# Attention's maxima and score products cut into eight tiles of 64 rows by 32 columns

## What is computed

```python
q = (x @ Wq.T + bq).reshape(Bb, Nn, H, hd).transpose(0, 2, 1, 3)
k = (x @ Wk.T + bk).reshape(Bb, Nn, H, hd).transpose(0, 2, 1, 3)
...
a1 = jax.nn.softmax(jnp.einsum('bhnd,bhmd->bhnm', q1, k1) * scale, axis=-1)
x1 = jnp.einsum('bhnm,bhmd->bhnd', a1, v1).transpose(0, 2, 1, 3).reshape(Bb, Nn, C // 2)
...
out = jnp.concatenate([x1 - lv * x2, x2], axis=-1) @ Wp.T + bp
```

## Time and profile before

| what | value |
|---|---|
| median of 3 runs | 4907.77 us |
| the profiled execution's own time | 4897.27 us |
| its span, first to last instruction | 4895.5 us |
| mean granted TensorE clock | 0.972 |
| TensorE busy (matmuls) | 4397.7 us, 90% |
| VectorE busy | 4273.3 us, 87% |
| ScalarE busy | 3642.8 us, 74% |
| POOL busy | 1583.7 us, 32% |

### The profile page before, as it was taken

How to read it: one execution, slowest core, us unless ns; L and a number is a source line. 1 busy time by engine, 2 the same in 40 slices (tenths; PEclk the granted TensorE clock), 3 DMA queues, 4 the chain that set the end, 5 groups by cost and what they waited for, 6 DMA issues and landing times. The chain is left out here.

```text
span 4895.5 us, 90703 instructions
## 1 busy us (share of the span) xinstructions
PE 4397.7 (90%) x33000; PEld 1847.3 (38%) x33000; DVE 4273.3 (87%) x5012; ACT 3642.8 (74%) x6131; POOL 1583.7 (32%) x1080
## 2 busy tenths in 40 slices
PE   6778778777876699999899999999999999999998
PEld 3225225224323355566433333333333333333335
DVE  5997998898898366555699999999999999999996
ACT  5766776676674333344599999999999999999993
POOL 0983893893895300000011111221101311131003
PEclk8999999999998899999999999999999999999998
DMA  2502101201201322221111111221112211222116
GB/s 76 171 0 100 39 1 51 88 1 36 85 1 35 132 91 70 69 87 61 46 35 34 41 36 43 52 53 34 36 35 57 56 36 35 53 54 73 24 29 194
DMA packets 371103, 275.37 MB, mean 56 GB/s; under 512 B 235795, under 2 KB 331886, under 8 KB 368814
## 3 DMA queue, kind: packets, MB, share of 16 engines
q1 hardware_dynamic: 330796, 166.29, 13.1%
q0 software_dynamic: 34720, 100.59, 6.4%
q10 hardware_dynamic: 5202, 3.18, 0.2%
HBM read 150.17 MB, written 118.69 MB: 55 GB/s over the span
## 5 line engine op out<-in xcount | busy, mean ns | idle before, releaser
L1785 DVE TENSOR_REDUCE at_mpart<-at_ps 128x1 f32<-128x1024 f32 x2048 | 2378.1, 1221 | 16.0 <-PE at_ps L1685 16.0
L1770 ACT ACTIVATE at_E<-at_ps 128x512 f32<-128x512 f32 x4096 | 2224.2, 596 | 133.7 <-PE at_ps L1694 21.4
L1701 PE MATMUL at_ps<-at_E,at_vst 128*32 128x256 f32 x16400 | 1311.1, 391 | 0.1
L1685 PE MATMUL at_ps<-at_ks,at_qs 48*128 48x512 f16 x4096 | 896.6, 434 | 14.9 <-DVE at_mpart L1785 14.9
L1694 PE MATMUL at_ps<-at_qs,at_ks 50*128 50x512 f16 x4096 | 782.5, 378 | 1.2 <-ACT at_E L1770 0.4
L1564 POOL DMA_INDIRECT at_y<-yd,at_gidx x128 | 132.5, 1035 | 1571.5 <-DVE at_mx L1790 1512.8
L1685 PEld LDWEIGHTS at_ps<-at_ks,at_qs 48*128 48x128 f16 x4096 | 293.6, 140 | 861.2 <-issue 735.1
L887 POOL TENSOR_TENSOR l_work<-l_work 128x1024 f32<-128x1024 f32 x252 | 593.8, 2356 | 34.0 <-issue 0.4
L783 PE MATMUL l_ps<-l_bc,l_sel 96*128 96x512 bf16 x1024 | 318.9, 396 | 248.8 <-DVE l_work L921 125.2
L1701 PEld LDWEIGHTS at_ps<-at_E,at_vst 128*32 128x32 f32 x16400 | 326.3, 108 | 552.5 <-issue 549.3
L819 PE MATMUL l_ps<-l_work,l_ident 128*128 128x512 f32 x1024 | 491.0, 601 | 5.1 <-DVE l_work L921 5.1
(11 more groups left out here) (263 smaller groups left out, 4179.9 us busy)
## 6 DMA issues: line engine op xcount, KB each, us to landing
xd<-l_zero SPq DMA_DIRECT2D x4, 5120.0 KB, 32.9
yd<-at_late POOLq DMA_DIRECT2D x40, 512.0 KB, 3.0
at_late<-xd POOLq DMA_DIRECT2D x38, 512.0 KB, 4.9
at_qs<-qp SPq DMA_DIRECT2D x132, 128.0 KB
at_ks<-kp SPq DMA_DIRECT2D x396, 32.0 KB
at_late<-in_eW SPq DMA_DIRECT2D x8, 1536.0 KB, 8.0
ot<-at_osb SPq DMA_DIRECT2D x516, 17.0 KB
at_qs<-qp SPq DMA_DIRECT2D x132, 64.0 KB
```

The source lines that it names most:

```text
L1685: mm = pe.matmul(ring[n % 2][:, r, :], peak_queries(m, row, buf, i), m.ks[row, buf, bass.ts(kh, BANK)], start=True, stop=True)
L1701: mm = pe.matmul(O[32 * q:32 * q + 32, :], m.vst[:, par, SLOTS_A * kk + sl, :], m.E[:, sl % 4, kk, bass.ts(q, QG)], start=(sl == 0 and kk ...
L1770: act.activation(m.E[:, sl % 4, kk, bass.ts(hf, BANK)], score_bank(t, 4 * sl + 2 * hf + kk), ACT.Exp, scale=scale).then_inc(s.ex, 1)
L1785: dve.tensor_reduce(m.mpart[:, half, job:job + 1], ring[n % 2].rearrange("p a b -> p (a b)"), AX_X, ALU.max).then_inc(s.ring_free, 1)
```

## The change

`peak` and `scores` each issue eight matmuls in place of two. Each row tile of 128 columns is cut into four column tiles of 32 columns, which write 32 partitions of the same PSUM bank. The moving operand, the banks, the waits and the increment after the last matmul stay as they are. The loop runs over the column tiles outside and the two row tiles inside. `values` and all other engines are not touched.

```diff
                 pe.wait_ge(s.ring_free, wait)
-                for r in range(2):
-                    row = slice(64 * r, 64 * r + STACK)
-                    mm = pe.matmul(ring[n % 2][:, r, :], peak_queries(m, row, buf, i), m.ks[row, buf, bass.ts(kh, BANK)], start=True, stop=True)
+                for c in range(4):
+                    for r in range(2):
+                        row, part = slice(64 * r, 64 * r + STACK), slice(32 * c, 32 * c + 32)
+                        mm = pe.matmul(ring[n % 2][part, r, :], peak_queries(m, row, buf, i)[:, part], m.ks[row, buf, bass.ts(kh, BANK)], start=True, stop=True)
                 mm.then_inc(s.ring, 1)
...
                 pe.wait_ge(s.ex, drained(t, l - 2))
-                for r in range(2):
-                    row = slice(64 * r, 64 * r + STACK + 2)
-                    mm = pe.matmul(score_bank(t, l + r), m.ks[row, j, bass.ts(sl, P)], m.qs[row, j, half * QB + hf * BANK:half * QB + (hf + 1) * BANK],
+                for c in range(4):
+                  for r in range(2):
+                    row, part = slice(64 * r, 64 * r + STACK + 2), slice(32 * c, 32 * c + 32)
+                    mm = pe.matmul(score_bank(t, l + r)[part, :], m.ks[row, j, sl * P + 32 * c:sl * P + 32 * c + 32], m.qs[row, j, half * QB + hf * BANK:half * QB + (hf + 1) * BANK],
                                    start=True, stop=True)
                 mm.then_inc(s.score, 1)
```

## The result

The changed kernel takes 4953.71 us (median of 4 runs, 4947.49 to 4959.47) against 4903.85 for the kernel before on the same chip (the three runs given above and a fourth): a ratio of 1.010 with a 95% interval of 1.0088 to 1.0112. That is 50 us slower, where 30 us faster was forecast. The time lies inside the stated range, and on the side that had a chance of 0.30.

A forecast was written before the change was run, and what follows sets the result against it. TensorE was taken to bound the kernel, VectorE close behind. Shorter jobs gave -39 us, late jobs +4, waits between the two engines +5: -30 us, 4867 us, or 4877 as a median. The range ran from 4838 to 4962.

The forecast's parts named there:

- What bounds: Attention jobs: TensorE sets the pace at 1.155 to 1.16 us a job, VectorE close behind at 1.13, ScalarE's floor 1.123.
- 1.123 us against 1.143: ScalarE in the attention: its work of 1.123 us a job fits within the new job of 1.143, counted at nothing.
- a quarter of 60, 15 ns: `peak`'s open load: 32 spread columns take 15 ns, a quarter of the 60 ns for 128 columns.
- slower, by the spread load: Rival at `peak`'s open load: each small load takes 60 ns, 47 us and 4 for late jobs, 4959 us; chance 0.20.
- Distance between tiles: `peak` and `scores` on TensorE: tiles start 3.8 ns apart, so the eighth starts 27 ns after the first.
- the feeding rival: Rival on TensorE: matmuls behind a wait come slower than 3.8 ns apart, some 600 us at most; chance 0.10, with no overlap.
- The waits between shapes: TensorE, `scores` to `values` and `values` to next `peak`: some 95 ns each at the change of tile shape, left unchanged.
- The sum: TensorE's job: last `scores` tile starts 27 + 15 + 215 = 257 ns after `peak` begins, against 279, 22 ns less.
- Edits at nothing: Counted at no cost: doubled instruction fetching stays hidden, `peak`'s end reaches VectorE 22 ns earlier, ScalarE waits as before.

The follow-up runs named there:

- early_again: Changed kernel with the first bank's four score tiles issued first and given an increment of their own: 4934.13 us, ratio 1.0059 to the kernel before.
- half_tiles: `peak` and `scores` cut into four tiles of 64 rows by 64 columns in place of eight of 64 by 32: 5040.47 us, ratio 1.0209.
- a_near: Changed kernel with every `peak` load reading adjacent queries, so maxima are of other queries: 4922.37 us, ratio 1.0031 to the kernel before.
- a_gaps: Changed kernel (eight tiles) with the queries that `peak` loads 8, 4, 2 and 1 elements apart, each on its own line: 4928.07 us in one run.

## Why the prediction was wrong

**What bounds.** Right for the kernel before. TensorE's sequence set the pace, with VectorE 25 ns behind. But ScalarE was weighed by its work, 1.123 us a job, and not by its chain. In the sum it stood as "1.123 us against 1.143". From the first score tile through its exponential to the next `scores` takes 0.49 + 0.65 = 1.14 us at the least in the kernel before, below TensorE's 1.157, and 0.54 + 0.65 = 1.19 in the long jobs after, above TensorE's 1.17. (The 0.49 is in the lines of the last section; 0.65 is the distance in the jobs after that waited.) This step failed. It is worth 15 ns on the average ordinary job, 1.169 us in early_again against 1.184, or 26 us over 1792 jobs, and the 21 us of early_again net. The 1.123 us was no floor either: it adds up records of 596 ns, while two exponentials in a row start 0.49 us apart (3058.91 and 3059.40 in the changed kernel).

**Loads.** The step "a quarter of 60, 15 ns" failed. A load of 32 spread columns takes 53 ns. The error was to read 60 ns for 128 columns as one column after another, on the strength of an f32 transpose with the same number in its row; it goes in four runs of 32 side by side, as far as the rows and the access pattern tell. What I had as a rival, "slower, by the spread load", had the right place and nearly the right price, 60 ns for a small load. Its reason was wrong: it made this "its price for each load and not for each column", and half_tiles shows a price for each column. Its total of 51 us met the measured 50 by luck, since the load gives only half of it. TensorE's own sequence lost 1.169 - 1.157 us = 12 ns a job (early_again against before), 25 us over 2048 jobs. With the 6 us of the third job this is about what early_again still loses, 4934.13 - 4905.25 = 29 us. The rest is ScalarE's chain.

**Distance between tiles.** Right: 3.3 ns against 3.8 taken. The Trainium skill's rule of 25 ns between the starts of matmuls (TensorE: Matmul & The Clock Gate, "Wait — 56ns, not 53.3ns?") does not hold between tiles here. With it the feeding rival falls. Tiles of both cuts run side by side: eight streams in 0.40 us.

**The waits between shapes.** Right: they stayed, at the same size.

**The sum.** With 53 ns in place of 15, the forecast's own formula gives 23 + 53 + 215 = 291 ns against 279. The difference, 12 ns, is what TensorE's sequence lost. With 15 ns and the chain as measured there would most likely still have been no gain: a_near, with 9 ns, has a ratio of 1.0031.

**The measured time in the range.** The range reached to 4962 for the sake of the spread-load rival. That 4953.71 lies in it is no merit of the forecast, which had the sign wrong.

**Edits at nothing.** The fetching was hidden, as said. The completion of the group was put down at no cost, and had one (below).

## What to carry to other kernels

Before a stationary operand is cut into column tiles, look at the access pattern of its load. A load of 128 columns may already run as four side by side, and then that of a quarter tile is no shorter (133 ns against 140 here), and that of a half tile is longer (189). A chain over another engine is measured from start to start, from the tiles to the release, and not by that engine's busy time, and where it equals the pace, every nanosecond on the last tile counts in full. Of two products of unlike loads in a row, try the order in which the expensive load stands behind a stream of the same tile shape, and see what the other engines then wait for: here the order alone gave 0.2%, and 0.6% with the copy moved ahead of the wait.

## What the runs showed of the hardware that was not expected

The completion of a group of eight tiles is seen later than that of two. In the timeline after, `scores` ends at 3058.37 + 0.40 = 3058.77 and its exponential starts at 3058.91, 0.14 us later. In the same place of the kernel before it is 0.11:

```profile
3012.48 0.38 PE L1694 MATMUL at_ps<-at_qs,at_ks 50*128 50x512 f16 x2
```

```profile
3012.97 0.60 ACT L1770 ACTIVATE at_E<-at_ps 128x512 f32<-128x512 f32 x1
```

With four tiles to an increment (early_again) the exponential starts at 3056.86, 0.50 us after the first score tile, in place of 0.54:

```profile
3056.86 0.60 ACT L1772 ACTIVATE at_E<-at_ps 128x512 f32<-128x512 f32 x1
```

Taken over the ordinary jobs of this kind in the traces, the median from the end of the last tile that the increment stands for to the start of the exponential is 107 ns for two tiles (before), 117 and 118 for four (early_again and half_tiles) and 138 for eight (after). That is 5 ns a tile. The Trainium skill has a tail of 4.7 ns a tile (TensorE: Matmul & The Clock Gate, The cost: per-tile semaphore tail). By it six tiles more would be 28 ns, an estimate. The 31 ns seen agree.

Why only every second job is long follows from a second difference. The exponential of the other jobs starts sooner, 0.48 us after `scores` in the changed kernel and 0.43 in the kernel before:

```profile
3011.32 0.38 PE L1694 MATMUL at_ps<-at_qs,at_ks 50*128 50x512 f16 x2
```

```profile
3011.75 0.60 ACT L1770 ACTIVATE at_E<-at_ps 128x512 f32<-128x512 f32 x1
```

So their chain takes 0.48 + 0.65 = 1.13 us and does not bind. In ScalarE's program the late ones are those of the first half of a slot, which stand behind one wait more (for `values`). Whether that is the reason no run tests.

Why a gap of 8 elements costs more than one of 4, and one of 2 almost nothing, is not settled here: in a_gaps the rows give 53, 23, 10 and 9 ns above the shortest load, and no run tried wider gaps.
